# The gathers of a second graph layer add into x by themselves

## The chip, the cores and the metric

The kernel runs on one core of one Trainium2 chip. The metric is the device time of one execution in microseconds, the median of the runs shown; lower is better.

## The reference

Four graphs (batch entries) of 512 tokens each have x of 512 values per token. A two-layer graph attention network over context features is followed by a mixture of experts with a shared expert. On this input the kernel's attention reduces to a gather: a token attends to the node whose index is the position of the largest value of x, and the output of the layers for that node is added to x.

```python
h = gat_layer(feats, adj, W0, a_self0, a_neigh0, b0)      # elu(alpha @ (feats @ W0) + b0)
h = gat_layer(h, adj, W1, a_self1, a_neigh1, b1)
...
scores = jax.nn.softmax(xf @ gate_w.T, axis=-1)
topk_w, topk_idx = jax.lax.top_k(scores, K)               # 6 of 64 experts, at most 128 tokens each
gu = jnp.einsum('ech,ehi->eci', gx, gate_up_proj)
hid = jax.nn.silu(g) * u
eo = jnp.einsum('eci,eih->ech', hid, down_proj) * buf_w[..., None]
shared = jax.nn.silu(xf @ shared_gate_w.T) * (xf @ shared_up_w.T) @ shared_down_w.T
return (routed + shared).reshape(b, s, h)
```

The experts work on x after the graph layers and a layer norm, so mean and variance of every token of x have to be known first.

## The kernel before

The 2048 tokens are 16 tiles of 128 (partitions) by 512, four tiles to a graph; graphs are numbered 0 to 3. Each engine has one program, written by hand in order, and semaphores tie them together. Nothing plans or reorders.

First part. For each tile n the layers run through all engines: TensorE multiplies (`first_layer`, `second_layer`, L592 and L604), ACT takes exponentials, VectorE finishes the second layer's row in `elu2` (tile `feat`), and SP stores that row to DRAM in `store_feat` (semaphore `feat_out`). `largest` finds each token's node; a first indirect DMA (`node_of_node`) turns it into the row number. When the four feature rows of a graph b have landed, POOL issues four indirect DMAs in `pick(b)`: each gathers 128 rows of 2 KB from DRAM into the buffer `picked`. VectorE's `add(b, tiles)` adds `picked` to `k.x` and takes `bn_stats` of the sum; `scale_of(b)` makes mean and variance; POOL's `scale(b)` raises the variance to the power -0.5; ACT's `norm` writes the normalised rows; TensorE transposes them and multiplies them by the gate (`gate`, `turn_logits`); VectorE's `choose`, `split_high` and `split_low` pick the experts and prepare the counting, until the table of tokens of each expert is written (L1237).

The order of what matters here is fixed. POOL: gathers of graph 2, four node gathers of graph 3, three additions of `count_seen(0)`, `scale(2)`, gathers of graph 3, `weigh(0)` with a store of gate weights, `count_seen(1)`, `scale(3)`. VectorE: `choose(1)`, `split_low(0)`, `add(3, ...)`, `scale_of(3)`, `choose(2)`. SP: the 16 feature rows, each followed by a store of zeros to the sums in DRAM (`clear`), then the weights of the first six experts, 768 and 384 KB each, which lie in the memory that the first part's buffers leave; SP therefore waits until the readers of those buffers are done, and one of these is the addition of `picked` (`x2_ready`).

Second part. For each of 64 experts POOL gathers the rows (L534), TensorE transposes and multiplies (L786, L806, L794), VectorE scales by the gate weight, and POOL scatters the result with an indirect DMA that adds in DRAM (L528). Weights of expert e are loaded when expert e - 6 is done.

Of the kernel before, what the change touches and what calls it, by code (L numbers as in the profile page):

```python
# [11 lines left out]
F32 = mybir.dt.float32  # L12
# [3 lines left out]
ALU = mybir.AluOpType  # L16
# [3 lines left out]
P = 128  # L20
B, N, D = 4, 512, 512
FIN, H, O = 128, 8, 64
T = B * N
NT = T // P
TB = N // P
# [70 lines left out]
def main_block(nc, k, a):  # L96
# [3 lines left out]
    with ExitStack() as ctx:  # L100
# [3 lines left out]
        def sem(name):  # L104
            return ctx.enter_context(nc.semaphore(name))
# [16 lines left out]
        node2 = sb("node2", [P, NT], U32)  # L122
# [5 lines left out]
        f = sb("f", [1, 16])  # L128
# [16 lines left out]
        with ExitStack() as first:  # L145
            def at(name, shape, dt=F32):
                return first.enter_context(nc.sbuf_tensor(name, shape, dt))

            w0 = at("w0", [P, H * O])
            w1 = at("w1", [P, H, KC, O])  # L150
            b1bc = at("b1bc", [P, H * O])
            ctxT = at("ctxT", [P, 2, N])
            h1T = at("h1T", [P, 2, KC, N])
            ex1 = at("ex1", [P, 2, N])
            s2 = at("s2", [P, 2, H * O])
            ex2 = at("ex2", [P, 2, H * O])
            feat = at("feat", [P, TB, H * O])
            picked = at("picked", [P, TB, H * O])
            with ExitStack() as early:
                nodes = early.enter_context(nc.sbuf_tensor("nodes", [P, NT, FIN], F32))  # L160
            rest_hi = at("rest_hi", [P, EG, SHI, 8], F16)
            rest_lo = at("rest_lo", [P, SLO, E], F16)
            cross = at("cross", [P, EG, SLO, 8], F16)
            cross2 = at("cross2", [P, EG, SLO, 8], F16)
            wts = at("wts", [P, 2, TB, E])
            seltok = at("seltok", [P, 2, TB, E], F16)
            lgT = at("lgT", [E, N])

            below = at("below", [P, TB, E])
            ex = at("ex", [P, TB, E])  # L170
            topc = at("topc", [P, TB])
            esum = at("esum", [P, TB])
            rsum = at("rsum", [P, TB])
            key = at("key", [P, TB, E + 2])
            ktop = at("ktop", [P, TB, 8])
            krep = at("krep", [P, TB, E + 2])
            sel = at("sel", [P, NT, E], F16)
            seen = at("seen", [P, B, E], F16)
            part = at("part", [P, 2, E], F16)
            hi = at("hi", [P, TB, E], F16)  # L180
            lo = at("lo", [P, TB, E], F16)
            ones_hi = at("ones_hi", [P, TB, EG, SHI, 8], F16)
            ones_lo = at("ones_lo", [P, TB, SLO, E], F16)
            rest = at("rest", [P, E], F16)
            resttok = at("resttok", [P, E], F16)
            rhi = at("rhi", [P, E], F16)
            rlo = at("rlo", [P, E], F16)

            rows = at("rows", [P, 2, TB, D])
# [21 lines left out]
        feat_out = [sem(f"feat_out{t}") for t in range(TB)]  # L211
        picked_in = [sem(f"picked_in{t}") for t in range(TB)]
        turn_done, turn_sb = sem("turn_done"), sem("turn_sb")
        l1_done, l1_exp, h1_ready = (sem(s) for s in ("l1_done", "l1_exp", "h1_ready"))
        l2_done, s2_ready, l2_exp, z2_ready, x2_ready = (sem(s) for s in ("l2_done", "s2_ready", "l2_exp", "z2_ready", "x2_ready"))
        absw_done, colsum_done, colsum_read = (sem(s) for s in ("absw_done", "colsum_done", "colsum_read"))
        abs_small, abs_nodes, squared, sq_ready, sq_rstd = (
            sem(s) for s in ("abs_small", "abs_nodes", "squared", "sq_ready", "sq_rstd"))
# [94 lines left out]
        with nc.Block() as block:  # L313
            @block.sync
            def _(sp):
# [62 lines left out]

                sp.wait_ge(l2_exp, NT)
                sp.wait_ge(z2_ready, NT)  # L380
                sp.wait_ge(x2_ready, NT)
                sp.wait_ge(abs_nodes, 2)
                for e in range(U):
                    load_expert(e)
# [18 lines left out]
            def _(pool):  # L403
# [52 lines left out]
                def pick(b):  # L456

                    pool.wait_ge(node2_in[b % 2], 16 * TB * (b // 2 + 1))
                    for t in range(TB):
                        pool.wait_ge(feat_out[t], 16 * (b + 1))  # L460
                    if b:
                        pool.wait_ge(x2_ready, b * TB)
                    for t in range(TB):
                        pool.indirect_dma_start(
                            picked[:, t, :], None, a[f"feat_dram{b}"],
                            bass.IndirectOffsetOnAxis(ap=node2[:, b * TB + t:b * TB + t + 1], axis=0)).then_inc(picked_in[t], 16)

                def scale(b):

# [542 lines left out]
            def _(dve):  # L1012
# [42 lines left out]
                        dve.wait_ge(b1_in, 16)  # L1055
                    nc.vector.tensor_tensor(s2[:, t % 2, :], L2[t % 2][:], b1bc[:], ALU.add).then_inc(s2_ready, 1)

                def add(b, tiles):

                    for t in tiles:  # L1060
                        n = b * TB + t
                        dve.wait_ge(picked_in[t], 16 * (b + 1))
                        dve.wait_ge(squared, n + 1)
                        nc.vector.tensor_tensor(k.x[:, n, :], k.x[:, n, :], picked[:, t, :], ALU.add).then_inc(x2_ready, 1)  # L1064
                    for t in tiles:
                        dve.wait_ge(x2_ready, b * TB + t + 1)
                        last = nc.vector.bn_stats(bn[:, t, :], k.x[:, b * TB + t, :])  # L1067
                    link(last)

# [110 lines left out]
                for n in range(NT):  # L1180
                    b, t = n // TB, n % TB
                    if n >= 2:
                        elu2(n - 2)
                    if b + 1 < B:
                        first_layer(b + 1, t)
                    for j in range(ahead[n], ahead[n + 1]):
                        largest(j)
                    if n == 2 * TB - 2:
                        dve.wait_ge(consts, 2)
                        nc.vector.memset(key[:], 1.0)  # L1190
                        nc.vector.tensor_reduce(k.same_e[:], k.ident[:].rearrange("p (a e) -> p e a", e=8), AX_X, ALU.add)
                    if n == 10:
                        dve.wait_ge(colsum_done, 1)
                        for j in range(2):
                            nc.vector.tensor_reduce(f[:, j:j + 1], CS[j][0:1, :], AX_X, ALU.max).then_inc(colsum_read, 1)
                    if n == 14:
                        dve.wait_ge(abs_nodes, 1)
                        nc.vector.tensor_reduce(rowstat[:, 0:1], nodes[:].rearrange("p t f -> p (t f)"),
                                                AX_X, ALU.max).then_inc(abs_nodes, 1)
                    second_layer(n)  # L1200
                    if n in (8, 12):
                        add(n // TB - 2, range(TB))
                        scale_of(n // TB - 2)
                    if n == 14:
                        choose(0)
                elu2(NT - 2)
                add(2, (0, 1))
                elu2(NT - 1)
                add(2, (2, 3))
                scale_of(2)  # L1210
                split_high(0)
                choose(1)
                split_low(0)
                add(3, range(TB))
                scale_of(3)
                choose(2)
                split_high(1)
# [433 lines left out]
```

## Time and profile before

| what | us |
|---|---|
| median of 3 runs (629.02 to 629.78) | 629.24 |
| the profiled execution | 630.29 |
| its span, first to last instruction | 627.6 |

The span is what the trace shows; 2.7 us of the profiled execution lie around it. Shares of the span: TensorE busy 91%, VectorE 42%, POOL 36%, ACT 26%. Times in the rows are microseconds from the start of the span. An engine's record can overlap the next one's by some 0.1 us.

### The profile page before, as it was taken

What the parts mean: (1) busy time and instruction counts of PE and PEld (TensorE: products, weight loads), DVE (VectorE), ACT (ScalarE), POOL (GpSimd) and SP (SyncE); (2) the same over time, 40 slices, a digit from 0 to 9 for tenths busy, and PEclk for the clock granted to TensorE, in tenths of its full rate; (3) what the DMA queues carried; (4) which work ended last, traced back from release to release, by engine and by line L of the source; (5) the groups of instructions that cost most, each with busy time, mean ns of one, the idle gap of its engine ahead of it and who ended that gap; (6) DMA issues with size and microseconds to landing.
All of it is one profiled execution on the core that took longest, in us unless ns stands there. A gap on an engine that the chain in (4) does not pass through costs nothing.

```text
span 627.6 us, 6138 instructions
## 1 busy us (share of the span) xinstructions
PE 570.0 (91%) x1967; PEld 300.0 (48%) x1967; DVE 262.6 (42%) x629; ACT 163.2 (26%) x342; POOL 226.2 (36%) x221
## 2 busy tenths in 40 slices
PE   5898997866689999999999999999999999999962
PEld 2444543333345555555555555555555555554320
DVE  0865789996412232223222332232222332323663
ACT  3765697662011111111111111111111111110000
POOL 3052157632054343434434434343343434422100
PEclk9999999978799999999999999999999999999967
DMA  8855387599038999998999999999899999953993
GB/s 286 308 200 171 105 281 267 194 302 298 13 113 239 275 300 287 255 298 250 275 268 283 272 286 300 281 276 269 245 267 285 270 280 296 292 119 41 305 386 142
DMA packets 47924, 155.02 MB, mean 247 GB/s; under 512 B 7760, under 2 KB 9296, under 8 KB 46224
## 3 DMA queue, kind: packets, MB, share of 16 engines
q1 hardware_dynamic: 29168, 109.74, 53.2%
q0 software_dynamic: 16320, 40.39, 26.8%
q10 hardware_dynamic: 2400, 4.46, 2.0%
q8 instruction: 17, 0.28, 0.2%
q14 instruction: 19, 0.16, 0.1%
HBM read 116.28 MB, written 38.28 MB: 246 GB/s over the span
## 4 chain that ended last, share of the span: by engine, by line
PE 76%; DVE 11%; issue 5%; DMA 4%; ACT 3%; POOL 0%; DVEq 0%; SPq 0%; POOLq 0%; ACTq 0%
PE bank L806 26%; PE bank L794 17%; PE bank L688 9%; PE bank L699 7%; PE bank L604 4%; PE bank L786 4%; DMA out<-y,table 2%; PE bank L592 2%; PE bank L818 2%; DVE ones_lo L1141 1%; DVE x L1064 1%; DMA w<-in_W 1%; DVE bn L1067 1%; DVE ones_hi L1134 1%; PE bank L613 1%
## 5 line engine op out<-in xcount | busy, mean ns | idle before, releaser
L806 PE MATMUL bank<-gu_w,gxT 128*128 128x384 f32 x512 | 175.7, 486 | 0.8 <-ACT gxT L995 0.8
L794 PE MATMUL bank<-dn_w,hidT 96*128 96x512 f32 x256 | 120.6, 593 | 0.9 <-DVE hidT L1295 0.9
L1276 DVE TENSOR_SCALAR y<-bank,gx 128x512 f32<-128x512 f32 x64 | 48.1, 751 | 165.8 <-PE bank L794 165.8
L806 PEld LDWEIGHTS bank<-gu_w,gxT 128*128 128x128 f32 x512 | 92.1, 190 | 51.9 <-issue 1.0
L1003 ACT ACTIVATE eg<-bank 128x192 f32<-128x192 f32 x64 | 21.2, 331 | 307.7 <-PE bank L806 307.7
L528 POOL DMA_INDIRECT out<-y,table x33 | 52.7, 1596 | 122.2 <-DVE y L1276 109.8
L688 PE MATMUL bank<-xnT,upT 128*128 128x512 f32 x192 | 90.1, 616 | 0.0
L528 POOL DMA_INDIRECT odd_sum<-y,table x31 | 49.1, 1582 | 105.8 <-DVE y L1276 99.0
L1290 DVE TENSOR_TENSOR hid<-bank,eg 128x192 f32<-128x192 f32 x64 | 31.8, 498 | 128.2 <-ACT eg L1003 119.5
L534 POOL DMA_INDIRECT gx<-rows_dram,table x64 | 63.4, 991 | 35.2 <-issue 16.8
L794 PEld LDWEIGHTS bank<-dn_w,hidT 96*128 96x128 f32 x256 | 45.7, 190 | 45.2 <-issue 43.7
L604 PE MATMUL bank<-w,h1T 128*128 128x512 f32 x128 | 57.8, 594 | 0.0
L688 PEld LDWEIGHTS bank<-xnT,upT 128*128 128x128 f32 x192 | 36.3, 198 | 38.3 <-issue 38.2
L699 PE MATMUL bank<-downT,shid 128*128 128x512 f32 x96 | 46.4, 627 | 7.5 <-DVE shid L1168 7.5
L786 PEld LDWEIGHTS bank<-ident,gx 128*128 128x128 f32 x256 | 32.0, 141 | 20.8 <-issue 12.5
L995 ACT ACTIVATE gxT<-bank 128x512 f32<-128x512 f32 x64 | 38.2, 597 | 6.8 <-PE bank L786 0.2
L786 PE MATMUL bank<-ident,gx 128*128 128x128 f32 x256 | 38.4, 273 | 0.2 <-DMA gx<-rows_dram,table 0.2
L604 PEld LDWEIGHTS bank<-w,h1T 128*128 128x128 f32 x128 | 23.8, 190 | 27.4 <-issue 26.2
L818 PEld LDWEIGHTS bank<-ident,hid 128*96 128x96 f32 x128 | 16.2, 127 | 35.0 <-issue 34.2
L699 PEld LDWEIGHTS bank<-downT,shid 128*128 128x128 f32 x96 | 18.3, 202 | 26.9 <-issue 18.6
L452 POOL DMA_INDIRECT node<-node_dram,node x16 | 17.1, 1071 | 30.0 <-DMA node_dram<-node 25.2
L1295 DVE COPY hidT<-bank 96x256 f32<-96x256 f32 x64 | 26.2, 410 | 0.5 <-PE bank L818 0.5
(175 smaller groups left out, 475.4 us busy)
## 6 DMA issues: line engine op xcount, KB each, us to landing
gu_w<-in_gate_up SPq DMA_DIRECT2D x64, 768.0 KB
dn_w<-in_down SPq DMA_DIRECT2D x64, 384.0 KB
x<-in_x SPq DMA_DIRECT2D x4, 1024.0 KB, 13.8
feat_dram<-feat SPq DMA_DIRECT2D x16, 256.0 KB, 3.0
out<-shid SPq DMA_DIRECT2D x8, 512.0 KB
odd_sum<-shid SPq DMA_DIRECT2D x8, 512.0 KB
rows_dram<-rows ACTq DMA_DIRECT2D x4, 1024.0 KB, 6.5
gu_w<-out SPq DMA_DIRECT2D x4, 1024.0 KB, 7.8
```

The costliest lines, as they stand in the source:

```text
L528: pool.indirect_dma_start(sums[lane(e)], bass.IndirectOffsetOnAxis(ap=table[:, e:e + 1], axis=0), y[:, e % YB, :], None, compute_op=ALU.ad ...
L534: pool.indirect_dma_start(gx[:, e % GX, :], None, a["rows_dram"][:, :], bass.IndirectOffsetOnAxis(ap=table[:, e:e + 1], axis=0)).then_inc( ...
L604: last = nc.tensor.matmul(L2[t % 2][:], h1T[:, b % 2, c, t * P:(t + 1) * P], w1[:, :, c, :], start=(c == 0), stop=(c == KC - 1))
L688: last = nc.tensor.matmul(UP[g][:], k.upT[:, c, g * SI + s * P:g * SI + (s + 1) * P], xnT[:, c, b * N:(b + 1) * N], start=(c == 0), stop=( ...
L699: last = nc.tensor.matmul(UP[t % 2][:], shid[b % 2][:, s, t * P:(t + 1) * P], k.downT[:, s, :], start=(s == 0), stop=(s == SC - 1))
L786: last = nc.tensor.transpose(GT[e % 2][:, c * P:(c + 1) * P], gx[:, e % GX, c * P:(c + 1) * P], k.ident[:])
L794: last = nc.tensor.matmul(DN[:], hidT[:, e % 2, j, :], dn_w[:, e % U, j, :], start=(j == 0), stop=(j == 1))
L806: last = nc.tensor.matmul(GU[e % 2][:, 0:2 * I], gxT[:, e % 2, c, :], gu_w[:, e % U, c, :], start=(c == 0), stop=(c == KC - 1))
L818: last = nc.tensor.transpose(HT[0:IH, j * P:(j + 1) * P], hid[:, j, :], k.ident[:])
L995: nc.scalar.activation(gxT[:, e % 2, :, :].rearrange("p c q -> p (c q)"), GT[e % 2][:], ACT.Copy).then_inc(gxT_ready, 1)
L1276: nc.vector.tensor_scalar(y[:, e % YB, :], DN[:], gx[:, e % GX, D + e:D + e + 1], None, ALU.mult).then_inc(y_ready, 1)
L1290: nc.vector.tensor_tensor(hid[:].rearrange("s j p -> s p j"), GU[e % 2][:, I:2 * I].rearrange("s (p j) -> s p j", j=2), eg[:].rearrange("s ...
```

## The change

The gather of `pick` names `k.x` as its destination and adds in flight (`compute_op=ALU.add`). VectorE's additions, the buffer `picked` and the semaphore `x2_ready` go; what is left of `add` is called `measure` and waits for each gather before its `bn_stats`. `nodes` takes the place of `picked` in memory. POOL now waits for ACT's squares of x (which read x before the addition) instead of the previous graph's additions, and SP, ahead of the weights, for the stores of the feature rows instead of the additions.

```diff
-            picked = at("picked", [P, TB, H * O])
-            with ExitStack() as early:
-                nodes = early.enter_context(nc.sbuf_tensor("nodes", [P, NT, FIN], F32))
+            nodes = at("nodes", [P, NT, FIN])
...
                 sp.wait_ge(l2_exp, NT)
                 sp.wait_ge(z2_ready, NT)
-                sp.wait_ge(x2_ready, NT)
+                for t in range(TB):
+                    sp.wait_ge(feat_out[t], 16 * B)
                 sp.wait_ge(abs_nodes, 2)
...
-                    if b:
-                        pool.wait_ge(x2_ready, b * TB)
+                    pool.wait_ge(squared, (b + 1) * TB)
                     for t in range(TB):
                         pool.indirect_dma_start(
-                            picked[:, t, :], None, a[f"feat_dram{b}"],
-                            bass.IndirectOffsetOnAxis(ap=node2[:, b * TB + t:b * TB + t + 1], axis=0)).then_inc(picked_in[t], 16)
+                            k.x[:, b * TB + t, :], None, a[f"feat_dram{b}"],
+                            bass.IndirectOffsetOnAxis(ap=node2[:, b * TB + t:b * TB + t + 1], axis=0),
+                            compute_op=ALU.add).then_inc(picked_in[t], 16)
...
-                def add(b, tiles):
+                def measure(b, tiles):
 
                     for t in tiles:
-                        n = b * TB + t
                         dve.wait_ge(picked_in[t], 16 * (b + 1))
-                        dve.wait_ge(squared, n + 1)
-                        nc.vector.tensor_tensor(k.x[:, n, :], k.x[:, n, :], picked[:, t, :], ALU.add).then_inc(x2_ready, 1)
-                    for t in tiles:
-                        dve.wait_ge(x2_ready, b * TB + t + 1)
                         last = nc.vector.bn_stats(bn[:, t, :], k.x[:, b * TB + t, :])
                     link(last)
```

On VectorE, at graph 3, behind the last `split_low(0)` instruction, the program had these rows before (`bn` holds the statistics, `mv` mean and variance):

```order
L1141 SCALAR_TENSOR_TENSOR ones_lo<-lo,seltok 128x4x64 x7
L1064 TENSOR_TENSOR x<-x,picked 128x512 [waits squared,picked_in0]
L1064 TENSOR_TENSOR x<-x,picked 128x512 [waits squared,picked_in1]
L1064 TENSOR_TENSOR x<-x,picked 128x512 [waits squared,picked_in2]
L1064 TENSOR_TENSOR x<-x,picked 128x512 [waits squared,picked_in3]
L1067 BN_STATS bn<-x 128x6 [waits x2_ready] x4
L1074 BN_AGGR mv<-bn 128x2 [waits vch]
```

The same place with the change:

```order
L1135 SCALAR_TENSOR_TENSOR ones_lo<-lo,seltok 128x4x64 x7
L1061 BN_STATS bn<-x 128x6 [waits picked_in0]
L1061 BN_STATS bn<-x 128x6 [waits picked_in1]
L1061 BN_STATS bn<-x 128x6 [waits picked_in2]
L1061 BN_STATS bn<-x 128x6 [waits picked_in3]
L1068 BN_AGGR mv<-bn 128x2 [waits vch]
```

The four additions are gone, and each `bn_stats` itself waits for its gather.

On POOL, from `scale(2)` to the store of graph 0's gate weights, before:

```order
L474 TENSOR_TENSOR rstd<-rstd,mhalf 128x4 [waits xn_ready,var_ready,seen_ready]
L475 TENSOR_TENSOR shift<-negmean,rstd 128x4 [waits pch]
L464 DMA picked<-feat_dram,node 128x512 [waits feat_out2,feat_out3,feat_out1,x2_ready,feat_out0,node2_in1]
L464 DMA picked<-feat_dram,node 128x512 x3
L493 TENSOR_TENSOR ex<-ex,sel 128x256 [waits exp_done,sel_ready]
L497 TENSOR_TENSOR wts<-ex,rsum 128x256 [waits rsum_ready,pch]
L501 DMA rows_dram<-wts 512x1x64 [waits wts_full]
```

With the change:

```order
L473 TENSOR_TENSOR rstd<-rstd,mhalf 128x4 [waits xn_ready,var_ready,seen_ready]
L474 TENSOR_TENSOR shift<-negmean,rstd 128x4 [waits pch]
L462 DMA x<-feat_dram,node 128x512 [waits feat_out2,feat_out3,feat_out1,squared,feat_out0,node2_in1]
L462 DMA x<-feat_dram,node 128x512 x3
L492 TENSOR_TENSOR ex<-ex,sel 128x256 [waits exp_done,sel_ready]
L496 TENSOR_TENSOR wts<-ex,rsum 128x256 [waits rsum_ready,pch]
L500 DMA rows_dram<-wts 512x1x64 [waits wts_full]
```

The order is the same; the gathers write x and wait for `squared` where they waited for `x2_ready`.

On SP, behind the last feature row and the last store of zeros, before:

```order
L332 DMA feat_dram<-feat 128x512 [waits z2_ready]
L337 DMA odd_sum<-shid 128x1024
L350 DMA gu_w<-in_gate_up 128x1536 [waits x2_ready,abs_nodes,z2_ready,l2_exp]
L351 DMA dn_w<-in_down 96x1024
L350 DMA gu_w<-in_gate_up 128x1536
```

With the change:

```order
L330 DMA feat_dram<-feat 128x512 [waits z2_ready]
L335 DMA odd_sum<-shid 128x1024
L348 DMA gu_w<-in_gate_up 128x1536 [waits feat_out2,feat_out1,feat_out3,feat_out0,abs_nodes,z2_ready,l2_exp]
L349 DMA dn_w<-in_down 96x1024
L348 DMA gu_w<-in_gate_up 128x1536
```

The first load of expert weights waits for the feature rows to be stored, no longer for the additions of graph 3.

## Rows read from the trace of the kernel before

**Rows 1.** Busy time by stretch: each engine (instructions), clock, DMA share, GB/s.
```profile
135.00:150.00 15.00, 12.85 (x74) 6.41 (x75) 10.27 (x45) 7.54 (x24) 2.46 (x4) 0.70 1.03 277
...
300.00:400.00 100.00, 100.00 (x337) 54.35 (x336) 28.79 (x54) 15.45 (x33) 41.24 (x32) 1.00 0.96 279
```

**Rows 2.** Chain of waits in order of time: start, us, what.
```profile
129.32 1.08 POOL rstd L474
...
172.36 0.20 DVE table L1237
```

**Rows 3.** Timeline of VectorE: start, us, line, operation.
```profile
88.14 2.49 DVE L1064 TENSOR_TENSOR x<-x,picked 128x512 f32<-128x512 f32 x4
...
118.96 4.64 DVE L1141 SCALAR_TENSOR_TENSOR ones_lo<-lo,seltok 128x256 f16<-128x256 f16 x8
123.53 2.59 DVE L1064 TENSOR_TENSOR x<-x,picked 128x512 f32<-128x512 f32 x4
126.05 2.46 DVE L1067 BATCH_NORM_STATS2 bn<-x 128x6 f32<-128x512 f32 x4
...
129.03 0.16 DVE L1079 TENSOR_SCALAR rstd<-mv 128x4 f32<-128x4 f32 x1
```

**Rows 4.** Timeline of ACT, normalisations of graph 3, idle time before in brackets.
```profile
130.72 4.43 ACT L887 ACTIVATE rows<-x,shift,rstd 128x512 f32<-128x512 f32 x4 [3.61 <-POOL shift L475]
```

**Rows 5.** Timeline of TensorE, around 83 us.
```profile
83.43 0.63 PE L582 MATMUL bank<-ident,rows 128*128 128x128 f32 x4 [0.94 <-ACT xnT L830]
```

**Rows 6.** Timeline of SP's queue: issues of DMAs.
```profile
94.32 0.32 SPq L332 DMA_DIRECT2D feat_dram<-feat  x1
...
108.88 0.32 SPq L332 DMA_DIRECT2D feat_dram<-feat  x1
...
126.27 0.33 SPq L350 DMA_DIRECT2D gu_w<-in_gate_up  x1
```

**Rows 7.** Timeline of POOL, gathers of graph 2 to gathers of graph 3.
```profile
97.56 1.01 POOL L464 DMA_INDIRECT picked<-feat_dram,node  x1 [2.08 <-DMA feat_dram<-feat]
...
102.66 0.95 POOL L452 DMA_INDIRECT node<-node_dram,node  x1 [0.30 <-issue]
...
109.81 0.64 POOL L486 TENSOR_TENSOR seen<-part 128x64 f16<-128x64 f16 x1
112.30 1.04 POOL L474 TENSOR_TENSOR rstd<-rstd,mhalf 128x4 f32<-128x4 f32 x1 [1.85 <-issue]
...
114.29 1.35 POOL L464 DMA_INDIRECT picked<-feat_dram,node  x1 [0.62 <-issue]
```

**Rows 8.** Instructions of L528, scatters that add: ns min/median/max.
```profile
L528 POOL DMA_INDIRECT out<-y,table x33: 1552/1583/2003, 189.1 to 586.7; - x33
```

**Rows 9.** One scatter alone: its issue, and DMA queues (packets, MB, share) in 562-564.5.
```profile
560.12 1.57 POOL L528 DMA_INDIRECT odd_sum<-y,table  x1 [3.38 <-DMA out<-y,table]
...
q0 software_dynamic: 143, 0.26, 80.2%
```

**Rows 10.** Scatter beside SP's loads: issues; queues in 579.6-583 (one row), 583-585 (two).
```profile
578.00 1.56 POOL L528 DMA_INDIRECT out<-y,table  x1 [2.95 <-DVE y L1276]
586.68 2.00 POOL L528 DMA_INDIRECT out<-y,table  x1 [7.12 <-DMA out<-y,table]
...
q1 hardware_dynamic: 465, 0.95, 91.4%
...
q0 software_dynamic: 122, 0.24, 65.8%
q1 hardware_dynamic: 157, 0.29, 43.2%
```

**Rows 11.** POOL's store of gate weights beside expert weights; queues in 133.1-137.5.
```profile
132.30 0.78 POOL L501 DMA_DIRECT2D rows_dram<-wts  x1 [0.29 <-POOL wts L497]
...
q1 hardware_dynamic: 259, 1.20, 103.9%
```

**Rows 12.** ACT's store of normalised rows, DMA queues in 113.5-116.4.
```profile
q10 hardware_dynamic: 525, 1.05, 96.7%
```

More of the change, by code:

```diff
@@ L214, in main_block @@
         l1_done, l1_exp, h1_ready = (sem(s) for s in ("l1_done", "l1_exp", "h1_ready"))
-        l2_done, s2_ready, l2_exp, z2_ready, x2_ready = (sem(s) for s in ("l2_done", "s2_ready", "l2_exp", "z2_ready", "x2_ready"))
+        l2_done, s2_ready, l2_exp, z2_ready = (sem(s) for s in ("l2_done", "s2_ready", "l2_exp", "z2_ready"))
         absw_done, colsum_done, colsum_read = (sem(s) for s in ("absw_done", "colsum_done", "colsum_read"))
@@ L1201, in _ @@
                     if n in (8, 12):
-                        add(n // TB - 2, range(TB))
+                        measure(n // TB - 2, range(TB))
                         scale_of(n // TB - 2)
@@ L1206, in _ @@
                 elu2(NT - 2)
-                add(2, (0, 1))
+                measure(2, (0, 1))
                 elu2(NT - 1)
-                add(2, (2, 3))
+                measure(2, (2, 3))
                 scale_of(2)
@@ L1213, in _ @@
                 split_low(0)
-                add(3, range(TB))
+                measure(3, range(TB))
                 scale_of(3)
```

## The prediction

> **What bounds the kernel now.** I read the table of stretches first, then the chain of waits in order of time, then the timelines of single engines between 85 and 135 us, and last the packets of the DMA queues in short stretches.
>
> The kernel has two parts. From about 178 us on, the experts run, and TensorE is busy all the time: 100.00 of 100 us at full clock, with the DMA engines at 0.96 [rows 1]. Nothing that the change touches runs there, so whatever time the first part gains or loses reaches the end unchanged. The first part ends when the table of tokens is written, at 172.36 us [rows 2]. The reader should see in the chain that its last leg begins with graph 3 (the last of four): POOL's power at 129.32 [rows 2], then ACT's four normalisations at 130.72, before which ACT had stood idle for 3.61 us [rows 4], then dependent steps on TensorE, ACT and VectorE to the table. POOL's power waits for VectorE's variance of graph 3, whose record starts at 129.03 [rows 3]. So the number to forecast is one: when the last bn_stats of graph 3 ends. Before, four adds began at 123.53 and four bn_stats at 126.05, and these ended at 126.05 + 2.46 = 128.51 [rows 3]. VectorE did not wait for the gathers then: the adds began 0.07 us before the previous group's record ended (118.96 + 4.64 = 123.60), so the gathers of graph 3 had landed in time.
>
> **The change, part by part.**
>
> *Adds that go.* Four blocks of four adds, 2.49 to 2.59 us each [rows 3]. The first lies beside a TensorE that hardly waits: the only gap it leaves is 0.94 us at 83.43, where TensorE waits for ACT's copy of a normalised row [rows 5]. I count 0.9 for it. The next two lie in VectorE's stretch without a pause from 88 on, and the fourth is at the place itself.
>
> *Start of the gathers of graph 2.* They waited for the last feature row of that graph, which SP sent at 94.32 and which had landed at 97.56, 3.24 us later [rows 6, 7]. The row is made on VectorE behind the second block of adds, so it comes 2.49 + 0.94 = 3.4 us earlier, and the gathers start at about 94.1.
>
> *Cost of issuing.* POOL took 1.01 us for a gather [rows 7]. No gather that adds is in the trace; the nearest row is the experts' scatter that adds, of the same 128 rows of 2 KB, at a median of 1.583 us [rows 8]. Bounds 1.0 and 1.6; I take 1.58, because adding is what the two have in common. With the 0.30 us between two of them, four take 7.5 us. The gathers of graph 2 then end at 101.6 (before: the next group at 102.66), the node gathers and the three additions of counts behind them take as long as before (102.66 to 109.81 + 0.64 = 110.45, so 7.8 us) and end at 109.4. POOL's power of graph 2, which before waited for VectorE until 112.30, can then start at once, since VectorE has lost two blocks by then. From it to the first gather of graph 3 took 114.29 - 112.30 = 1.99 us [rows 7]. So the gathers of graph 3 start at 111.4 instead of 114.29. The new wait on ACT's squares costs nothing: it is cover by order, the squares of a graph stand in ACT's queue ahead of the feature rows for which POOL waits anyway.
>
> *The weights come forward.* SP held the first 12 loads of expert weights (6.75 MB) until all adds were done: first one at 126.27 [rows 6]. Now they wait only for the last feature row, sent at 108.88 before. It comes earlier by something between nothing and the two blocks ahead of it, 5.0 us; I take 1.5, because TensorE and ACT, which feed it, gain less than VectorE. With 3.24 us to land, that is 110.6. The other new cover: `nodes`, which now lies where weights will land, was last read before the additions of graph 2, and SP still waits for that (`abs_nodes`). The table ends long after the weights are in, so this gains nothing by itself. But it puts 6.75 MB in front of, and beside, the four gathers of graph 3, and VectorE now stands still until they land; behind its wait are graph 3's variance, and behind that POOL, ACT and TensorE in the order told above.
>
> *What a gather that adds costs the DMA engines.* Alone: a scatter issued at 560.12 to 561.69 has its packets between 562 and 564.5, 143 packets, 80.2% of 16 engines for 2.5 us, so 2.0 us of all engines [rows 9]. Beside a long queue: the scatter issued at 578.00 to 579.56 sends no packet before 583; until then the other queue alone runs, at 91.4%. Then the two queues share: 122 packets against 157 in 2 us, so its 144 packets need 2.4 us, up to 585.4; the next scatter, which waits for its landing, starts only at 586.68, so with POOL's usual 0.30 us ahead of an issue a landing takes 1.0 [rows 10]. The same under the weights themselves: the store of the gate weights, issued from 132.30 to 133.08, has no packet up to 137.5 while 259 packets of weights go out, of 1.20/259 MB = 4.6 KB each, each 103.9% x 4.4 us x 16 / 259 = 0.28 us of an engine [rows 11]. So POOL's queue waits 3.4 to 4.4 us behind a queue that is full, and then goes packet by packet with it.
>
> *The sum.* First gather of graph 3 issued at 111.4 + 1.58 = 113.0. First packet 3.4 to 4.4 us later: 116.9 in the middle. Each gather has 8 rows on each engine. The price of one gather: lower bound 2.0 us, as alone [rows 9]; beside small packets 2.4 [rows 10]; upper bound 8 x (0.173 + 0.28) = 3.6, a row that adds, 65.8% x 2 us x 16 / 122 = 0.173 us, in turns with a packet of weights, 0.28 [rows 10, 11]. The weights are what will lie beside it, so I take the middle of the last two, 3.0; four make 12.0. Last packet: 116.9 + 12.0 = 128.9. Landing 1.0, last bn_stats 0.67: 130.6, against 128.51. **The kernel becomes 2.1 us slower.** The profiled execution would go from 630.29 to 632.4; its own time lies 1.05 above the median of the runs, so the median goes from 629.24 to 631.3. ACT's store of graph 1's normalised rows (1 MB, 525 packets of 96.7% x 2.9 us x 16 / 525 = 0.085 us [rows 12]) comes out at about the same time as the weights; I count it at nothing, since it starts ahead of the gathers, and at 0.085 for each of 16 rounds, 1.4 us, if it is still there. VectorE is ready for graph 3 at 118.5 to 121 (123.53 less two blocks, or less one where its other waits, for the logits of graph 1, take their place [rows 3]), so it waits some 9 us for the last gather, and the additions saved are paid back in waiting.
>
> **The rivals.**
>
> *A, the other side: the queue is not held.* The weights don't delay the gathers, which land as fast as POOL issues them: last issue ends at 111.4 + 4 x 1.58 + 3 x 0.30 = 118.6, last packet 2.8 us later (561.69 to 564.5 [rows 9]), 121.4; bn_stats end at 123.1, 5.4 us earlier. ACT cannot use all of it: its idle time was 3.61 us [rows 4], more only as far as its own earlier work moves too. Middle 4.5: 624.7. For it: in the experts' part gathers, scatters and weights keep up with TensorE at a DMA share of 0.96 [rows 1]. Against it: the two holds [rows 10, 11]. The sign turns when the last packet is out before 126.8.
>
> *B, turns from the first packet.* No hold of 3.4 to 4.4 us, the queues alternate at once: 113.3 + 12.0 = 125.3, bn_stats end at 127.0, 1.5 us earlier: 627.7. Against it: the two holds [rows 10, 11]. The Trainium skill, "DMA: Bandwidth & Descriptors", section "Queues, rings and completion order", says that each DMA engine goes round the queues that have work, a packet from each; by that alone rival B's 627.7 would be the time. The trace agrees with the taking of turns, once POOL's queue has begun (122 against 157 packets), not with its beginning at once.
>
> *C, hold, but cheap turns.* 2.0 to 2.4 us for each gather, because a sum into on-chip memory may be cheaper than one into DRAM: last packet at 124.9 to 126.5, the end 126.6 to 128.2, that is 0.3 to 1.9 us earlier, about 628.1.
>
> *D, each of the four is held anew.* 4 x (3.4 + 2.4) = 23.2 after 113.0: 136.2, the end at 137.9, 9.4 us later: 638.6. For it: the trace shows the hold for single transfers only [rows 10, 11]; against it: they are issued 1.9 us apart, so the next one is in the queue before the one ahead has ended.
>
> *E, the picks of earlier graphs stall VectorE too.* Those of graph 2 start at 94.1 and need four times 2.0 to 2.4 us behind SP's stores of zeros; VectorE wants the first at about 104, so a stall stays below 1 us and is in the range.
>
> **How the numbers follow.** The forecast's mechanism has 0.50, A 0.16, B 0.08, C 0.14, D 0.12. A difference of 0.2% (1.26 us) is about what a measurement of this kernel can tell from none. The forecast's own range, with holds and turns at their bounds, is 629.5 to 633.5; about 0.10 of its 0.50 falls within 0.2%. Faster: A 0.16, most of B 0.05, a part of C 0.04: 0.25. Within: 0.10 of the forecast, 0.03 of B, 0.10 of C: 0.23. Slower: 0.40 and D 0.12: 0.52. To leave out no more than 2 in 10, the range reaches to A's better half and short of D's middle: 625.5 to 635.5.
>
> **What would show it.** In the profile after: no TENSOR_TENSOR on x with picked; a gather on POOL of 1.6 us; the first weights at about 110.6; graph 3's gathers at about 111.4, the first packet of POOL's queue 3 to 4 us after its issue; VectorE idle for 5 to 12 us before the bn_stats of graph 3, released by the gathers; the last bn_stats ending near 130.6; the experts' part of the same length. I am wrong if VectorE doesn't wait there (A), if the gathers' packets begin beside the weights at once (B), or if TensorE's clock, 0.70 in 135 to 150 us of the profile of before [rows 1], moves to its other level in the legs behind graph 3.

## The result and the profile after

The changed kernel takes **637.82 us** (median of 4 runs, 637.12 to 638.38) against 629.51 us (629.02 to 630.35) of the kernel before beside it: ratio 1.013, 95% interval 1.0113 to 1.0148. Slower was forecast, but 631.3 with a range up to 635.5; the loss is four times the size.

The chain of waits of the changed kernel, in order of time (start, us, what), answers to [rows 2]:

```profile
138.51 1.08 POOL rstd L473
...
147.54 5.25 PE bank L612 x8
...
179.68 0.20 DVE table L1231
```

POOL's power for graph 3 starts 138.51 - 129.32 = 9.19 us later than in [rows 2]. The table is written at 179.68 instead of 172.36, 7.32 us later, and the span is 7.3 longer (634.9 for 627.6). So all of the loss is there before 138.51, and the leg behind it even gave 1.87 us back. The stretches (columns as in [rows 1]) show what changed in it:

```profile
135.00:150.00 15.00, 6.56 (x19) 3.75 (x20) 12.70 (x60) 8.88 (x17) 4.55 (x9) 0.57 0.86 260
150.00:165.00 15.00, 9.87 (x83) 5.42 (x82) 11.40 (x50) 4.63 (x20) 3.85 (x6) 0.96 0.23 80
300.00:400.00 100.00, 100.00 (x337) 54.36 (x336) 28.20 (x53) 16.03 (x34) 41.18 (x32) 1.00 0.95 276
```

The experts' stretch is as before. The middle of the leg now lies in the second of these rows, where TensorE's clock was granted at 0.96, behind a stretch in which TensorE was busy 6.56 of 15 us (1.00 is the upper of the clock's two levels, 2.4 GHz; a smaller mean mixes in the lower, 1.2 GHz). The leg's eight multiplications by the gate take 5.25 us above. The kernel before had a clock of 0.77 in that stretch, and the multiplications took 6.47 us:

```profile
150.00:165.00 15.00, 9.11 (x60) 4.56 (x58) 8.42 (x41) 1.69 (x10) 1.79 (x3) 0.77 0.45 164
```

```profile
138.35 6.47 PE bank L613 x8
```

Now the cause of the 9.19 us. The timeline of VectorE after (start, us, line; in brackets the idle time ahead and what ended it), its bn_stats for graphs 1, 2 and 3:

```profile
92.39 0.69 DVE L1061 BATCH_NORM_STATS2 bn<-x 128x6 f32<-128x512 f32 x1 [3.44 <-DMA x<-feat_dram,node]
...
109.83 0.69 DVE L1061 BATCH_NORM_STATS2 bn<-x 128x6 f32<-128x512 f32 x1 [1.58 <-DMA x<-feat_dram,node]
126.75 0.69 DVE L1061 BATCH_NORM_STATS2 bn<-x 128x6 f32<-128x512 f32 x1 [5.99 <-DMA x<-feat_dram,node]
129.36 0.69 DVE L1061 BATCH_NORM_STATS2 bn<-x 128x6 f32<-128x512 f32 x1 [1.92 <-DMA x<-feat_dram,node]
133.96 0.69 DVE L1061 BATCH_NORM_STATS2 bn<-x 128x6 f32<-128x512 f32 x1 [3.90 <-DMA x<-feat_dram,node]
137.00 0.69 DVE L1061 BATCH_NORM_STATS2 bn<-x 128x6 f32<-128x512 f32 x1 [2.35 <-DMA x<-feat_dram,node]
```

Four blocks of adds (some 10 us) are gone [rows 3], and VectorE waits 3.44 + 1.58 + 14.16 = 19.2 us for gathers in their place. The last bn_stats ends at 137.69, against 128.51. POOL's timeline, the first gather of graph 2 and the first and last of graph 3, with the wait for the gathered node numbers ahead (answers to [rows 7]):

```profile
97.62 1.64 POOL L462 DMA_INDIRECT x<-feat_dram,node  x1 [2.06 <-DMA feat_dram<-feat]
...
115.00 1.64 POOL L462 DMA_INDIRECT x<-feat_dram,node  x1 [2.15 <-DMA node<-node_dram,node]
...
120.81 1.55 POOL L462 DMA_INDIRECT x<-feat_dram,node  x1 [0.30 <-issue]
```

SP's first weights, 126.27 before [rows 6]:

```profile
114.30 0.33 SPq L348 DMA_DIRECT2D gu_w<-in_gate_up  x1
```

The DMA queues (packets, MB, share of 16 engines; q0 is POOL's, q1 SP's, q10 ACT's), from 117 to 120 us and from 121 to 137 us:

```profile
q1 hardware_dynamic: 197, 0.99, 98.5%
q10 hardware_dynamic: 29, 0.05, 4.0%
```

```profile
q1 hardware_dynamic: 688, 3.22, 57.0%
q0 software_dynamic: 608, 1.15, 36.6%
q10 hardware_dynamic: 353, 0.72, 11.9%
```

The first issue ends at 116.64. Up to 120 POOL's queue has no row: its first packet comes at about 120.3, some 3.6 us after the issue's end; ACT's store and then the weights fill the engines up to there. From then on it sends in every microsecond, about as many packets as the weights, until the last gather has landed at 137.0.

### The profile page after: what moved, and what is told of

It reads as the page before. It is cut to its first block, busy times and chain, and to the rows that moved or that the text cites. A ratio compares the mean times of both kernels' runs of the same rounds, so it can differ in the third digit from the quotient of the medians.

```text
span 634.9 us, 6108 instructions
## 1 busy us (share of the span) xinstructions
PE 570.9 (90%) x1967; PEld 301.2 (47%) x1967; DVE 251.2 (40%) x613; ACT 162.7 (26%) x342; POOL 233.1 (37%) x221
## 3 DMA queue, kind: packets, MB, share of 16 engines
HBM read 116.28 MB, written 38.28 MB: 243 GB/s over the span
## 4 chain that ended last, share of the span: by engine, by line
PE 75%; DMA 9%; DVE 4%; issue 4%; POOL 3%; ACT 2%; DVEq 0%; SPq 0%; POOLq 0%; ACTq 0%
PE bank L805 26%; PE bank L793 17%; PE bank L687 9%; PE bank L698 7%; PE bank L603 5%; PE bank L785 4%; DMA out<-y,table 3%; POOL x L462 2%; DMA x<-feat_dram,node 2%; PE bank L591 2%; PE bank L817 2%; DMA feat_dram<-feat 1%; DMA w<-in_W 1%; DVE ones_lo L1135 1%; PE bank L612 1%
## 5 line engine op out<-in xcount | busy, mean ns | idle before, releaser
L603 PE MATMUL bank<-w,h1T 128*128 128x512 f32 x128 | 59.3, 607 | 0.0
L462 POOL DMA_INDIRECT x<-feat_dram,node x16 | 25.9, 1619 | 16.9 <-DMA feat_dram<-feat 11.1
```

The lines of the kernel that those rows point to most:

```text
L462: pool.indirect_dma_start(k.x[:, b * TB + t, :], None, a[f"feat_dram{b}"], bass.IndirectOffsetOnAxis(ap=node2[:, b * TB + t:b * TB + t + 1 ...
L603: last = nc.tensor.matmul(L2[t % 2][:], h1T[:, b % 2, c, t * P:(t + 1) * P], w1[:, :, c, :], start=(c == 0), stop=(c == KC - 1))
```

## The experiments

Two words first. The hold is the time from the end of the first issue to the first packet of POOL's queue; turns are two or more queues sending packet for packet. Theory 1: the loss comes from the weights that came forward, which hold POOL's queue and then take turns with it. Theory 2: a gather that adds is slow in itself. Theory 3: the loss arises upstream, in the waits for graphs 1 and 2 and for the node numbers, beside SP's stores of zeros. All ratios are to the kernel before, measured beside each run.

**Weights behind the gathers.**

```diff
-                    sp.wait_ge(feat_out[t], 16 * B)
+                    sp.wait_ge(picked_in[t], 16 * B)
```

> The changed kernel, but SP sends the first weights only when all gathers of graph 3 have landed, instead of when its last feature row has landed. Theory 1 (the loss comes from the weights that came forward: POOL's queue is held behind them and then takes turns with them): POOL's queue sends its first packet within 2 us of the first issue, a gather needs about 2.1 us, the last one lands near 124 us, the last bn_stats of graph 3 ends near 125 (128.51 before, 137.69 in the changed kernel), and the time is 625 to 628 us. Theory 2 (a gather that adds is slow in itself, 4.1 us whatever lies beside it): the last bn_stats ends at 134 or later, 634 to 638 us. Theory 3 (the loss arises upstream, in the waits for graphs 1 and 2): the time stays above 634 us.

Measured: 624.74 us, ratio 0.9939 (0.9914 to 0.9963), faster than the kernel before and just below the time expected. VectorE's last two bn_stats of graph 3:

```profile
124.07 0.69 DVE L1061 BATCH_NORM_STATS2 bn<-x 128x6 f32<-128x512 f32 x1 [1.66 <-DMA x<-feat_dram,node]
126.27 0.69 DVE L1061 BATCH_NORM_STATS2 bn<-x 128x6 f32<-128x512 f32 x1 [1.51 <-DMA x<-feat_dram,node]
```

Moving the weights alone, with the same gathers, turns +1.3% into -0.6%. Theory 2 falls as a cause of the loss. The last bn_stats ends at 126.96, two microseconds later than expected.

**Plain gathers, weights early.** The kernel before, with

```diff
...
-                sp.wait_ge(x2_ready, NT)
+                for t in range(TB):
+                    sp.wait_ge(feat_out[t], 16 * B)
                 sp.wait_ge(abs_nodes, 2)
                 for e in range(U):
-                    load_expert(e)
+                    load_up(e)
+                    if e < 4:
+                        load_down(e)
+                sp.wait_ge(x2_ready, NT)
+                for e in range(4, U):
+                    load_down(e)
```

> The kernel before, with its plain gathers and its adds, but the weights come forward as in the change: SP sends the first weights when the last feature row has landed (the two loads whose buffers share memory with the gathers' buffer still wait for the adds). Theory 1: plain gathers of graph 3 are held 3.4 to 4.4 us behind the weights too and then take turns with them at 2.5 to 3 us each; VectorE waits before its adds of graph 3, the last bn_stats ends at 131 to 134 instead of 128.51, and the time is 632 to 635 us. Theory 2 (the gather that adds is what is slow): plain gathers land in time, 629.5 us, no change.

Measured: 631.34 us, ratio 1.0043 (1.0026 to 1.0061). The direction is theory 1's, the size below it: the last add starts at 126.99, the last bn_stats ends at 130.07.

```profile
126.99 0.69 DVE L1077 TENSOR_TENSOR x<-x,picked 128x512 f32<-128x512 f32 x1 [0.86 <-DMA picked<-feat_dram,node]
```

The queues from 119 to 127 us show why plain gathers lose less:

```profile
q1 hardware_dynamic: 337, 1.68, 59.0%
q0 software_dynamic: 337, 1.11, 42.1%
```

The turns are exact, 337 against 337, but POOL's packets are larger: 1.11 MB/337 = 3.3 KB, where the adding ones have 1.15/608 = 1.9 KB. The same megabyte takes fewer turns. So early weights cost a third of the loss even with plain gathers (1.0043 of 1.013). The rest came only with gathers that add: by their smaller packets, as argued here, and by the delay upstream that the next run shows.

**Zeros early.** The changed kernel, with

```diff
+                zeros_at = {n: range(2 * n, 2 * n + 2) for n in range(5)}
+                zeros_at[5], zeros_at[6] = range(10, 13), range(13, NT)
                 for n in range(NT):
                     store_feat(n)
...
-                    clear(n)
+                    for m in zeros_at.get(n, ()):
+                        clear(m)
```

> The changed kernel, but SP's stores of zeros into the buffers of sums, one behind each feature row, stand two and three at a time behind the feature rows of graphs 0 and 1, so none lies beside the gathers of graphs 1 to 3. Theory 3 (the loss arises upstream: those zeros delay the gathers of graph 1 and the node gathers of graph 3): the waits of 3.44 and 1.58 us on VectorE shrink below 1 us, the gathers of graph 3 start at about 111.5, and the time falls to 631 us or below. Theory 1: the same earlier start, but the weights come as much earlier, the gathers are still held and take 4.1 us each; the time is 633 to 636 us.

Measured: 633.23 us, ratio 1.0075 (1.0047 to 1.0104). VectorE no longer waits for graphs 1 and 2, and the gathers of graph 3 start at 111.06:

```profile
111.06 1.64 POOL L465 DMA_INDIRECT x<-feat_dram,node  x1 [0.16 <-issue]
```

```profile
120.73 0.69 DVE L1064 BATCH_NORM_STATS2 bn<-x 128x6 f32<-128x512 f32 x1 [3.38 <-DMA x<-feat_dram,node]
...
132.97 0.69 DVE L1064 BATCH_NORM_STATS2 bn<-x 128x6 f32<-128x512 f32 x1 [3.62 <-DMA x<-feat_dram,node]
```

From the end of the first issue (112.70) to the landing of the last gather (132.97) it is 20.3 us; in the changed kernel 137.00 - 116.64 = 20.4. So the 3.9 us of earlier start come out whole, and the gathers stay as slow. Theory 3 holds for that part (1.0130 to 1.0075), theory 1 for the rest.

**Zeros early and weights behind the gathers.** Both edits.

> Both edits together: zeros early, and the weights behind the gathers of graph 3. Theory 1: the gathers of graph 3 start at about 111.5 and land by 121, VectorE hardly waits for them, the last bn_stats ends at 122 to 124, and the time is 623 to 626 us, below the kernel before. Theory 2: 632 us or more. Theory 3: about the time of the run with zeros early alone.

Measured: 620.30 us, ratio **0.9874** (0.9835 to 0.9914), the best version here, and below the 623 to 626 us expected.

```profile
123.10 0.69 DVE L1064 BATCH_NORM_STATS2 bn<-x 128x6 f32<-128x512 f32 x1 [0.63 <-DMA x<-feat_dram,node]
```

The last bn_stats ends at 123.79, 4.72 us before that of [rows 3]; the span is 9.3 us shorter. Most of the rest comes out of the leg behind: 38.76 us from POOL's power (124.62) to the table (163.38), where the kernel before had 43.04. In the two stretches from 120 us

```profile
120.00:135.00 15.00, 11.79 (x72) 5.77 (x71) 14.06 (x63) 12.15 (x28) 7.07 (x15) 1.00 0.93 298
135.00:150.00 15.00, 9.87 (x83) 5.34 (x82) 12.54 (x51) 4.78 (x22) 5.02 (x6) 0.95 1.02 342
```

TensorE's clock was granted at 1.00 and 0.95, where the kernel before had 0.70 in the second [rows 1], and the chain's eight multiplications by the gate take

```profile
132.83 3.66 PE bank L615 x8
```

instead of 6.47. Why the clock stays up is not shown. The leg's start alone does not settle it: with POOL's power at 125.30 these multiplications took 3.66 us (*One expert early*), at 126.59 they took 6.61 (*Weights behind the first gather*), and at 129.13, as in the kernel before, 5.06 (*Zeros early, old gathers*). So about half of this version's gain lies in the leg, 2.81 us of it in these multiplications alone, and differences of a few microseconds between the runs hold some of the clock too.

**Zeros early, old gathers.** The kernel before with the edit of the zeros alone.

> The kernel before, plain gathers and adds on VectorE, with only SP's stores of zeros moved early. If the gain of zeros early together with late weights (0.9874) belongs to the gathers that add, this run shows no change, within 0.3% of the kernel before, because VectorE did not wait for any gather from 88 us on. If it belongs to the zeros, this run gains 3 to 5 us as well (ratio 0.992 to 0.995).

Measured: 628.80 us, ratio 0.9981 (0.9966 to 0.9996): nearly nothing, as in the first reading. The gain of the best version needs gathers that add.

**Weights to follow the issue.** The best version, with SP waiting for a semaphore that POOL raises behind its fourth gather:

```diff
...
-                for t in range(TB):
-                    sp.wait_ge(picked_in[t], 16 * B)
+                sp.wait_ge(picks_issued, 1)
...
+                    if b == B - 1:
+                        pool.sem_inc(picks_issued, 1)
```

> Gathers that add, zeros early, and SP sends the weights as soon as POOL has issued the last gather of graph 3 (not when it has landed), so no weights are queued ahead of the gathers but they lie beside the last ones. If a hold arises only behind weights that were queued first: the first packet of POOL's queue comes within 2 us of the first issue, the two last gathers take turns with the weights at up to 4.1 us each, the last bn_stats of graph 3 ends at 124 to 127, and the time is 621 to 624 us, ratio 0.988 to 0.994. If any weights hold POOL's queue for 3.5 us, whenever they come, the last bn_stats ends at 128 or later, ratio 0.997 or more.

Measured: 630.35 us, ratio 1.0001 (0.9983 to 1.0018). It answers a different question, since the weights did not follow the issue. SP's first weights and POOL's last gather:

```profile
111.50 0.33 SPq L349 DMA_DIRECT2D gu_w<-in_gate_up  x1
```

```profile
115.93 1.55 POOL L465 DMA_INDIRECT x<-feat_dram,node  x1 [0.30 <-issue]
```

The weights started 6 us before the last issue ended. So it is one more run with weights beside all four gathers (the last bn_stats ends at 130.21), and it decides nothing about weights that come second; the run with the weights behind the first gather does that.

What it adds is a comparison with *Zeros early* (1.0075), which also has weights beside all four gathers. POOL's first packet came at 116.5 here, 4.6 us after the first issue's end, 2.1 of them behind ACT's store of rows alone; there it came at 116.1, after 3.4. Yet from the first packet to the last landing it took 129.52 - 116.5 = 13.0 us here and 132.97 - 116.1 = 16.9 there. Beside some 620 packets of POOL's lay ACT's packets, in *Zeros early* from 116 to 133 us, then here from 116 to 130 us:

```profile
q10 hardware_dynamic: 695, 1.39, 21.5%
```

```profile
q10 hardware_dynamic: 189, 0.39, 7.2%
```

That is 3.7 us of all engines against 1.0. So a third queue takes turns too, and 2.7 of the 3.9 us between the two can be put down to it by this working; the weights differ less (707 and 653 packets).

**Smaller packets of weights.** The changed kernel, the first six gate and up weights in two halves:

```diff
-                    sp.dma_start(gu_w[:, u, :, :], a["gate_up"][e].rearrange("(p c) n -> p c n", c=KC)).then_inc(w_in[u], 16)
+                    whole = a["gate_up"][e].rearrange("(p c) n -> p c n", c=KC)
+                    for c in ((0, KC // 2), (KC // 2, KC)) if e < U else ((0, KC),):
+                        sp.dma_start(gu_w[:, u, c[0]:c[1], :], whole[:, c[0]:c[1], :]).then_inc(w_in[u], 16)
...
-                    pe.wait_ge(w_in[e % U], 32 * (e // U + 1))
+                    pe.wait_ge(w_in[e % U], 32 * (e // U + 1) + 16)
```

> The changed kernel, but the first six gate and up weights are loaded in two halves each, with packets of half the length; the same bytes are loaded at the same place. If the price of a gather is its number of packets times the sum of its own packet and one packet of weights (the queues take turns by packets), the packets of weights fall from about 0.28 us to about 0.19, a gather that adds costs 3.2 to 3.5 us instead of 4.1, the last bn_stats of graph 3 ends 2.5 to 3.5 us earlier than 137.69, and the ratio is 1.007 to 1.010. If the queues share the engines by bytes or by time, nothing changes: ratio 1.012 to 1.014.

Measured: 632.01 us, ratio 1.004 (1.0019 to 1.006), a larger gain than expected. The queues from 121 to 126 us, first in the changed kernel, then here:

```profile
q1 hardware_dynamic: 220, 1.03, 63.1%
q0 software_dynamic: 212, 0.40, 43.4%
```

```profile
q0 software_dynamic: 299, 0.55, 59.1%
q1 hardware_dynamic: 301, 0.89, 49.0%
```

Both times the queues send packet for packet (212 and 220, 299 and 301). With packets of weights of 0.89 MB/301 = 3.0 KB instead of 1.03/220 = 4.7 KB, POOL's queue gets 299/212 = 1.41 times as many in the same time. The last bn_stats waits until 131.76:

```profile
131.76 0.69 DVE L1063 BATCH_NORM_STATS2 bn<-x 128x6 f32<-128x512 f32 x1 [3.09 <-DMA x<-feat_dram,node]
```

From the first issue's end to the last landing it is 131.76 - 114.89 = 16.9 us instead of 20.4, the 3.5 that were expected at most; another 1.75 us come from gathers that started earlier (113.25), with the same program up to there.

**Weights behind the first gather.** The best version with

```diff
-                for t in range(TB):
-                    sp.wait_ge(picked_in[t], 16 * B)
+                sp.wait_ge(picked_in[0], 16 * B)
```

> Gathers that add, zeros early, and SP sends the weights when the first gather of graph 3 has landed; the other three are in POOL's queue by then, so no weights are queued ahead of them, and the weights lie beside the last two. If weights hold POOL's queue only when they were queued first: POOL's queue keeps sending without a break once the weights begin, its last two gathers take turns at about 3.1 us each (as with two queues in the run in which the weights were to follow the issue), the last bn_stats of graph 3 ends at 124.5 to 126.5 (123.8 with weights behind all gathers), ratio 0.989 to 0.993. If weights hold it whenever they come: a break of over 3 us in POOL's packets, the last bn_stats at 127 or later, ratio 0.995 or more.

Measured: 625.62 us, ratio 0.9922 (0.9901 to 0.9943), with the last bn_stats ending at 125.76, both as expected if only weights queued first hold POOL's queue:

```profile
125.07 0.69 DVE L1063 BATCH_NORM_STATS2 bn<-x 128x6 f32<-128x512 f32 x1 [4.09 <-DMA x<-feat_dram,node]
```

The queues from 115 to 118 us, then from 119 to 125 us:

```profile
q0 software_dynamic: 279, 0.51, 103.0%
```

```profile
q1 hardware_dynamic: 283, 1.38, 68.3%
q0 software_dynamic: 184, 0.38, 31.7%
```

POOL's queue falls from 93 packets in a microsecond to 31, but doesn't stop: from its first packet (113.5, behind ACT's store) to 125 us there is no microsecond in which it sends nothing. So weights that come second did not hold it here; weights queued first did in the runs above. VectorE waits 4.09 us for the fourth gather, more than the 3.1 us expected for one.

**One expert early.** The changed kernel with

```diff
-                for e in range(U):
-                    load_expert(e)
+                load_expert(0)
+                for t in range(TB):
+                    sp.wait_ge(picked_in[t], 16 * B)
+                for e in range(1, U):
+                    load_expert(e)
```

> The changed kernel, but only the weights of one expert (1.15 MB of 6.75) come forward; the other five experts' follow the landing of graph 3's gathers. The first packet of POOL's queue comes as late as in the changed kernel, 3.5 to 4 us after the first issue ends, and then the gathers run alone at 2.0 to 2.1 us each. If the loss of 1.3% is mostly turns with the weights: the last bn_stats of graph 3 ends at 128.5 to 130.5 instead of 137.69, ratio 0.998 to 1.002. If it is mostly the hold: it ends at 133 or later, ratio 1.006 or more.

Measured: 625.98 us, ratio 0.9939 (0.9917 to 0.9962), below what either reading expected.

```profile
120.00 0.69 DVE L1064 BATCH_NORM_STATS2 bn<-x 128x6 f32<-128x512 f32 x1 [2.02 <-DMA x<-feat_dram,node]
121.26 0.69 DVE L1064 BATCH_NORM_STATS2 bn<-x 128x6 f32<-128x512 f32 x1 [0.57 <-DMA x<-feat_dram,node]
122.51 0.69 DVE L1064 BATCH_NORM_STATS2 bn<-x 128x6 f32<-128x512 f32 x1 [0.55 <-DMA x<-feat_dram,node]
123.79 0.69 DVE L1064 BATCH_NORM_STATS2 bn<-x 128x6 f32<-128x512 f32 x1 [0.59 <-DMA x<-feat_dram,node]
```

The hold is there: the first issue ends at 113.85, and the first packet follows 2.6 us later, when most of the expert's weights are out. But the gathers that piled up behind it then land 1.26 us apart, faster than POOL issues them, and the last has landed 9.9 us after the first issue's end. With no weights in the way it took 126.27 - 116.28 = 10.0. **Of the two, the hold costs nothing here, where the gathers run alone behind it: the turns do.** In the changed kernel the gathers took 20.4 us, 10.5 more; at most 3.6 of these are the hold, which there stands ahead of the turns. What it costs there, no run separates.

In one table, each from the end of the first issue of graph 3 to the start of what waits for the last gather, in the profiled executions:

| Kernel | First issue starts | To the last landing | Ratio |
|---|---|---|---|
| Changed kernel | 115.00 | 20.4 | 1.0130 |
| Zeros early | 111.06 | 20.3 | 1.0075 |
| Small packets of weights | 113.25 | 16.9 | 1.0040 |
| Plain gathers, weights early | 113.28 | 12.4 | 1.0043 |
| Weights behind the first gather, zeros early | 109.87 | 13.6 | 0.9922 |
| Weights to follow the issue (they did not), zeros early | 110.24 | 17.6 | 1.0001 |
| One expert early | 112.21 | 9.9 | 0.9939 |
| Weights behind the gathers | 114.39 | 10.0 | 0.9939 |
| Weights behind the gathers, zeros early | 111.59 | 9.8 | 0.9874 |

## Why the prediction was wrong

**Right:** the direction, the place (VectorE's wait before the bn_stats of graph 3), and the mechanism. The adds that go are paid back in waiting for gathers that stand behind the weights and then take turns with them. *Cost of issuing* was 1.54 to 1.68 us for 1.58. The hold was 3.6 to 3.7 us, within 3.4 to 4.4. The experts' part kept its length. Not right was the time in *The weights come forward*: 110.6, where it was 114.30.

The forecast had the last bn_stats of graph 3 ending at 130.6; it ended at 137.69, 7.1 us later. Two terms make this up: the start of the gathers, and the price of one gather.

**The failed step: "so the gathers of graph 3 start at 111.4".** They started at 115.00, 3.6 us late. Behind it stand two steps upstream. Rival E's "a stall stays below 1 us" looked only at the picks of graph 2. VectorE waited 3.44 us for graph 1's last gather, which took back the 3.4 us of *Start of the gathers of graph 2* (97.62, where 94.1 was forecast), and 1.58 us for graph 2's. And "the node gathers and the three additions of counts behind them take as long as before" overlooked their landing: POOL stood 2.15 us for the numbers. With the zeros early, *Zeros early* has none of the three waits, and its gathers of graph 2 start at 94.11, the forecast's 94.1; in *Zeros early and weights behind the gathers* 0.70 us for graph 1 is left. In the four kernels that add in flight with zeros early the gathers of graph 3 start between 109.87 and 111.59, around the forecast's 111.4; so SP's stores of zeros are what delayed them. How long these waits are varies: in the four kernels with one program up to there (the changed one, *Weights behind the gathers*, *Smaller packets*, *One expert early*), the wait for graph 1 was 3.44, 0.42, 0.79 and 1.50 us, the one for graph 2 1.58, 2.80, 1.50 and 2.05, and the gathers of graph 3 started at 115.00, 114.39, 113.25 and 112.21. So the step failed by 0.8 to 3.6 us, and the changed kernel's profile shows the most.

**The mis-sized term: "3.0; four make 12.0".** From the first packet (120.3) to the last landing (137.0) it took 16.7 us, for which the forecast had 12.0 + 1.0: 3.7 us more, and the hold was some 0.2 shorter than the 3.9 taken. 3.6 + 3.7 - 0.2 = 7.1. The price of a turn was known: 0.173 + 0.28 = 0.453 us [rows 10, 11]. After, it is worked out from the queues' shares from 121 to 137 us: 0.154 us for POOL's packet, 688/608 packets of weights at 57.0% x 16 us x 16 / 688 = 0.212, and 353/608 packets of ACT's store at 0.086, together 0.44. That 0.453 and 0.44 agree is in part luck: a packet of weights cost less than the 0.28 taken, and ACT's store, which the sum left out, made up for it. Two choices made 12.0 of it: the middle between this price and that beside small packets was taken, although the weights were named as what would lie there, and eight packets for each engine were counted. [Rows 9] had 143 packets, nine for each engine. Four gathers of nine turns at 0.453 are 16.3 us, with the landing 17.3, where 16.7 were seen. The Trainium skill, "DMA: Bandwidth & Descriptors", section "The descriptor swizzle", gives eight data pairs and a completion for each engine to one software-generated transfer of 1 MiB to 128 partitions. The 143 packets of [rows 9] agree with nine; a plain gather, with 80 (last section), has five.

ACT's store of rows, "counted at nothing" or 1.4 us, was there from 128 us on: 36 turns x 353/608 x 0.086 = 1.8 us. This share is worked out; no run leaves that store out, but *Weights to follow the issue* beside *Zeros early* points the same way.

**The rivals.** *D* gave the nearest time, 638.6, by a mechanism that was not there: the queue is held once, then sends in every microsecond. *B* fails by the hold: behind weights queued first POOL's queue got no turn for 2.6 to 4.6 us in six kernels. The section of the Trainium skill that it named, "Queues, rings and completion order" in "DMA: Bandwidth & Descriptors", has each engine go round its queues by whole packets, of some 9 to 17 descriptors each. The trace agrees with the turns once both queues send, 299 packets against 301; how many descriptors one of its packets holds, it does not show. *C* fails in the changed kernel, though a gather that adds is cheaper than its lower bound: in *One expert early* three landed 1.25 to 1.26 us apart from 120.00 on, with next to nothing beside them, not 2.0. *A* is what happens without the weights: it forecast that bn_stats end at 123.1, and with zeros early and weights behind the gathers they end at 123.79.

**The leg behind.** The prediction named a change of TensorE's clock there as what would make it wrong. It moved, to the good side: 41.17 us from POOL's power to the table instead of 43.04, so 9.2 us of delay became 7.3 of span. The forecast had no term for this.

## What to carry to other kernels

Taking work off an engine can also remove a wait that held back somebody else's transfers. Here the adds' semaphore was what kept 6.75 MB of weights out of the gathers' way, and the change gave 0.6% once another wait kept that order, 1.3% once the stores of zeros were out of its way too (about half of that in the leg behind, at a faster clock). Price a small-packet transfer beside a large-packet queue by turns, its packets (completions too) times one packet of each queue, and not by its bytes; and before counting on an earlier start, follow the small transfers upstream, for whatever fills the engines beside them.

## What the runs showed of the hardware

- A gather of 128 rows of 2 KB sends 144 packets when it adds and 80 when it doesn't. POOL's queue with four gathers and one store of gate weights, first adding (*Zeros early and weights behind the gathers*, 114 to 124 us), then plain (*Zeros early, old gathers*, 116 to 124 us):

```profile
q0 software_dynamic: 624, 1.18, 74.6%
```

```profile
q0 software_dynamic: 368, 1.18, 54.3%
```

  The plain four alone are 320 packets (116 to 122 us), so the store has 48.
- POOL's queue got no packet out for 2.6 to 3.9 us behind weights queued first, in five kernels (the changed one, plain gathers, zeros early, small packets, one expert early), and for 4.6 us in *Weights to follow the issue*, at first behind ACT's store. Behind ACT's store alone it was 1.5 us (*Zeros early and weights behind the gathers*) and 2.0 (*Weights behind the first gather*), with nothing ahead 0.7 (*Weights behind the gathers*). Nor is the hold POOL's alone: in *Zeros early* ACT's store, issued by 109.87, had its first packet at 113.5, 3.7 us later, behind the weights sent from 108.84 on. When the weights came second, POOL's queue did not stop once. What sets the length of a hold stays open.
- In *Weights to follow the issue* a semaphore that POOL's program raises behind its fourth indirect DMA released SP's weights at 111.50, 6 us before the profile's row of that DMA ended (117.48).
